# A two-layer gated cross-attention and expert kernel: another order for the two passages from attention to experts

## The reference, cut to what matters

```python
x = x + tanh(g_xattn[0]) * L0_xattn(layernorm(x), ctx)         # 8 heads of 64
x = x + tanh(g_ffn[0])   * L0_experts(layernorm(x))            # silu(a) * b, biases, top 2 of 8
x = x + tanh(g_xattn[1]) * L1_xattn(layernorm(x), ctx, ctx)    # 16 heads of 8
x = x + tanh(g_ffn[1])   * L1_experts(layernorm(x))            # gelu, top 2 of 8
```

## Time and profile before

| | |
|---|---|
| median of 3 runs | 788.54 us (787.5 to 790.2) |
| profiled execution | 795.85 us, of which the span of the instructions is 794.1 us |
| granted TensorE clock, mean | 0.933 |
| busy share of the span | PE 81%, DVE 70%, POOL 56%, ACT 56% |
| layer 0 attention | row minima from 36.2 to 232.1 us |
| layer 0 experts | first block's PE product at 247.5 us, last store at 419.7 us |
| layer 1 attention | row maxima from 414.9 to 640.7 us |
| layer 1 experts | first block's PE product at 655.5 us, last store at 779.0 us |

### The profile page before, as it was taken

How to read it: one execution, slowest core, us unless ns; L and a number is a source line. 1 busy time by engine, 2 the same in 40 slices (tenths; PEclk the granted TensorE clock), 3 DMA queues, 4 the chain that set the end, 5 groups by cost and what they waited for, 6 DMA issues and landing times.

```text
span 794.1 us, 16522 instructions
## 1 busy us (share of the span) xinstructions
PE 647.0 (81%) x4501; PEld 584.0 (74%) x4501; DVE 556.0 (70%) x1971; ACT 442.0 (56%) x1275; POOL 448.4 (56%) x665
## 2 busy tenths in 40 slices
PE   6888888899766767978688899889879875898886
PEld 5677778888666657877677788878768874787775
DVE  3367688887874566876787889888878755444564
ACT  2476767677434434655556776767665542433452
POOL 4035357776667565875445334767656665565541
PEclk9999999998978788999997999999999996999999
DMA  9446667454422223434352435535413013332444
GB/s 261 117 115 171 174 172 182 124 154 110 127 72 87 62 79 113 110 93 119 106 156 76 114 78 107 122 85 103 113 58 84 31 34 93 102 89 79 135 145 153
DMA packets 127383, 89.48 MB, mean 113 GB/s; under 512 B 30996, under 2 KB 116276, under 8 KB 127260
## 3 DMA queue, kind: packets, MB, share of 16 engines
q1 hardware_dynamic: 110844, 64.93, 32.1%
q0 software_dynamic: 8128, 17.65, 6.8%
q10 hardware_dynamic: 8320, 5.85, 2.6%
HBM read 50.73 MB, written 39.85 MB: 114 GB/s over the span
## 4 chain that ended last, share of the span: by engine, by line
PE 39%; DVE 21%; issue 12%; ACT 11%; SPq 5%; another core or an unknown queue 4%; DMA 3%; POOL 2%; DVEq 1%; ACTq 0%; POOLq 0%
PE banks L1171 7%; PE banks L1191 5%; PE banks L1034 5%; SPq L824 3%; DMA v_rows<-vo 3%; DVE row_max L1428 3%; PE banks L914 2%; PE banks L1001 2%; PE banks L977 2%; PE banks L1212 2%; PE banks L1019 2%; DVE hidden L1743 2%; DVE up L1735 2%; DVE x_res L1767 2%
## 5 line engine op out<-in xcount | busy, mean ns | idle before, releaser
L1925 POOL DMA_INDIRECT y_rows<-y_sb,result_at x134 | 131.1, 978 | 107.9 <-DVE result_at L1723 46.5
L1171 PE MATMUL banks<-xb,up 128*128 128x128 f32 x820 | 127.8, 297 | 47.1 <-DVE hidden L1743 22.4
L1171 PEld LDWEIGHTS banks<-xb,up 128*128 128x128 f32 x820 | 112.8, 207 | 61.5 <-issue 33.7
L1918 POOL DMA_INDIRECT x_rows<-xm,row x120 | 120.5, 1004 | 31.6 <-issue 28.5
L1880 POOL TENSOR_TENSOR v_flat<-v_raw,row_head 104x64 f32<-104x64 f32 (+1 forms) x128 | 55.6, 461 | 73.1 <-ACT v_raw L1345 72.1
L1191 PE MATMUL banks<-down,hidden 128*128 x536 | 87.6, 289 | 8.9 <-DVE y_sb L1760 4.6
L1329 ACT ACTIVATE prob_t<-banks 128x512 f32<-128x512 f32 x192 | 73.3, 439 | 28.7 <-PE banks L1001 24.8
L1034 PE MATMUL banks<-v_flat,prob_t 128*128 128x108 f32 (+2 forms) x640 | 86.5, 284 | 3.3 <-ACT prob_t L1329 1.3
L1034 PEld LDWEIGHTS banks<-v_flat,prob_t 128*128 128x128 f32 (+1 forms) x640 | 79.7, 197 | 10.6 <-ACT prob_t L1329 6.8
L1383 ACT ACTIVATE gate<-banks,block_bias 128x128 f32<-128x128 f32 x142 | 44.4, 365 | 76.2 <-PE banks L1171 44.7
L1191 PEld LDWEIGHTS banks<-down,hidden 128*128 128x128 f32 x536 | 75.0, 202 | 12.0 <-issue 12.0
(11 more groups left out here) (238 smaller groups left out, 1657.9 us busy)
## 6 DMA issues: line engine op xcount, KB each, us to landing
vo_flat<-v_rows SPq DMA_DIRECT2D x32, 256.0 KB
x_norm<-x_rows SPq DMA_DIRECT2D x74, 72.0 KB
v_rows<-vo SPq DMA_DIRECT2D x38, 128.0 KB
x_far<-x_rows SPq DMA_DIRECT2D x60, 72.0 KB
gathered<-y_rows ACTq DMA_DIRECT2D x32, 128.0 KB
q_rows<-up_raw SPq DMA_DIRECT2D x8, 512.0 KB, 2.8
q_even<-q_rows SPq DMA_DIRECT2D x12, 256.0 KB
q_odd<-q_rows SPq DMA_DIRECT2D x12, 256.0 KB
```

What stands on the lines that cost most here:

```text
L1171: done = pe.matmul(banks[:, UP_BANK[i % 2], part * P:(part + 1) * P], block_w[:, i % WR, part // 2, part % 2 * P:(part % 2 + 1) * P], xb[: ...
L1918: pool.indirect_dma_start(out=x_rows[layer][:, :], out_offset=bass.IndirectOffsetOnAxis(ap=row[:, n, c:c + 1], axis=0), in_=xm[:, i % 2, j ...
L1925: pool.indirect_dma_start(out=y_rows[layer][:, :], out_offset=bass.IndirectOffsetOnAxis(ap=result_at[:, i % (2 * YR):i % (2 * YR) + 1], ax ...
```

## The change

Only places in the task list change; no instruction is added or removed. With g for the group:

- Layer 0, part 0: totals from u = 27 to 28; the pieces of the table from 28, 28, 28 to 29, 30, 30; the bias product from 29 to 31.
- Layer 0, leads: group 5 from u = 32 to 35, group 6 from 35 into the experts' list, group 7 later in that list. In the list the order before is route tasks of group 7, totals, scatters, lead, three pieces with the last scatters between them, bias. After: the same without the lead, then bias, lead 6, lead 7 (steps 24 and 26 in place of 15 for lead 7).
- Layer 1, part 0: totals from u = 44 to 45; the pieces from 45, 45, 45 to 46, 47, 48.
- Layer 1, scatters of group 5: from u = 61, 62, 63, 64 to 61, 64, 64, 64.
- Layer 1, part 1: totals from u = 66, and the three pieces from u = 67, into the experts' list: totals at s = 5, pieces at 7, 9 and 11, between the tasks of the dense group. Group 6's lead goes from u = 67 to s = 13.
- Layer 1, dense group: its statistics from s = 5 to u = 68; its lead and `expert_w` from s = 15 to 14. The list no longer has rests in layer 1.

```diff
@@ expert_steps
-            rest = step[-1][0] != "scatter"
+            rest = layer == 0 and step[-1][0] != "scatter"
@@ order
-    steps0 = [((0, 1, 2, 3, 4, 5, 6), (5, 6, 7, 8))] * 5 + [((0, 1, 2, 3, 4, 5, 6), (5, 6, 7, 8)), ((0, 1, 2, 3, 3, 4, 5), (5, 5, 5, 5)), ((0, 1, 2, 3, 4, 5, 6), (5, 6, 7, 8))]
-    steps1 = [((0, 1, 3, 5, 6, 7, 9), (9, 11, 13, 15))] * 5 + [((0, 1, 3, 5, 6, 7, 9), (8, 9, 10, 11)), ((0, 1, 2, 3, 4, 5, 6), (6, 6, 7, 7)), ((0, 1, 3, 5, 6, 7, 9), (9, 11, 13, 15))]
-    tasks = [route_tasks(0, GS, 6, steps0, ((5, (6, 6, 6), 7), (5, (6, 6, 6), 7))),
-             route_tasks(1, 2 * GS, 13, steps1, ((7, (8, 8, 8), 0), (5, (6, 6, 6), 0)))]
+    steps0 = [((0, 1, 2, 3, 4, 5, 6), (5, 6, 7, 8))] * 5 + [((0, 1, 2, 3, 4, 5, 9), (5, 6, 7, 8)), ((0, 1, 2, 3, 3, 4, 14.5), (5, 5, 5, 5)), ((0, 1, 2, 3, 4, 5, 10.6), (5, 6, 7, 8))]
+    steps1 = [((0, 1, 3, 5, 6, 7, 9), (9, 11, 13, 15))] * 5 + [((0, 1, 3, 5, 6, 7, 9), (8, 11, 11, 11)), ((0, 1, 2, 3, 4, 5, 17), (6, 6, 7, 7)), ((-1, 1, 3, 5, 7, 0, 9), ())]
+    tasks = [route_tasks(0, GS, 6, steps0, ((6, (7, 8, 8), 9), (6, (7, 8, 9), 10))),
+             route_tasks(1, 2 * GS, 13, steps1, ((8, (9, 10, 11), 0), (8, (10, 12, 14), 0)))]
```

## The result

The change makes the kernel faster, by half of what was forecast: 787.11 us median (779.07 to 789.25, 20 runs) against 790.02 us (786.11 to 795.53, 20 runs), ratio 0.9942, 95% interval 0.9919 to 0.9965. The ratio is that of the means (785.77 and 790.34 us): 4.6 us less, with 1.9 either way. The medians differ by 2.9 alone, since after has a tail of short executions, down to 779.07. Timed twice more, each time beside the kernel before on one chip, the same kernel had 0.9942 (0.9917 to 0.9967) and 0.9963 (0.9940 to 0.9986).

The account below looks back on a forecast made before the run. No engine fills the span (PE 81%, DVE 70%), so waits that change by stage bound the kernel. Terms -1.4, 0, -3.0 and -4.2 sum to -8.6 us: 787.2 from the profiled 795.85, carried to the median 779.9; range 771 to 790.

Parts of the forecast that it names:

- the tables of layer 1: Layer 1's attention, part 0: totals and pieces moved into steps with waits, plus 0.5 for PE's clock; -3.0 us, ends -5.9 and 0.
- the passage: Layer 1, from last attention steps into the experts: four terms, -1.6, -4.1, +1.5 and 0, summing to -4.2 us.
- (a): Layer 1 passage: with group 5's scatters behind the last values, PE's product starts 1.6 us earlier; ends 0 and -1.6.
- (c): Layer 1 experts, steps 5 to 11: the moved 5.9 us of totals and pieces mostly fit DVE's free time; +1.5, ends 0 and 5.9.
- Layer 0: -1.4: End of layer 0's attention: totals, pieces and bias moved later, sum -1.4 us, ends -2.9 and +1.5.
- experts 0 (+-2): Layer 0's experts: scatters, pieces and bias one step earlier, leads 6 and 7 later; 0 us, ends -2 and +2.
- (d): Layer 1 experts: no rests, earlier expert_w and later leads touch nothing waited for before step 21's dense products; 0 us.
- trains of scatters: Rival, layer 1 passage: a train of six scatters holds PE's results, rank 2.5 us later; 792.5 us, slower; chance 0.15.
- (b): Layer 1 passage: without the lead behind totals, POOL starts group 6's eight scatters 4.1 us earlier; -4.1, bounds -6 and +1.
- shut out by DVE: Rival, layer 1 experts: POOL's stores grow beside DVE's table instructions, at most 1.7 us lost; 781.6 us; chance 0.03.
- Given back: Rival: gains hold up to the last attention step, but (b) is 0 and (c) is 4; 786.5 us; chance 0.17.
- more: Rival, layer 1: split train releases PE's results 6 us earlier and (c) is free; -12.0, with table ends 775; chance 0.15.

Follow-up runs that it names:

- 790 sets: The timed sets, the result among them, in which the kernel before takes 790 to 794 us; the 790 level is theirs.
- pair of traces: The two profiled executions against each other: kernel before 795.85 us, changed kernel 787.56 us.
- 745 sets: The two follow-up sets, first and fourth, in which the same kernel before takes 745 us.
- second set: Follow-up runs of the changed kernel and three variants of it, beside a kernel before of 792.17 us; the changed kernel 0.9942.
- third and fifth set: Third: variants combined, and group 6's lead by itself, kernel before 794.34 us. Fifth: changed kernel again (0.9963), and with totals at u = 44 (0.9943), kernel before 794.08.
- s3: Kernel before with layer 1's part 0 pieces at u = 46, 47, 48 and totals left at u = 44: 742.62 us, ratio 0.9954.
- p2: Kernel before with only layer 1's part 0 tables moved (totals u = 45, pieces 46, 47, 48): 744.78 us, ratio 0.9994.
- p3: Kernel before with the passage of layer 1 alone changed: 742.19 us, ratio 0.9956.
- s2: Kernel before with all of layer 1's part of the change, layer 0 as before: 739.81 us, ratio 0.9925.
- p4: Changed kernel with group 5's scatters back at one pair a step, u = 61 to 64: 740.71 us, ratio to before 0.9958.
- s4: Kernel before with layer 1's part, but totals at u = 44 and scatters of groups 5 and 6 one pair a step: 740.39 us, ratio 0.9947.
- q4: Changed kernel with scatters one pair a step, group 5's at u = 61 to 64, group 6's at 67 to 70: 785.72 us, ratio to before 0.9920.
- r1: Changed kernel with layer 1's part 0 totals at u = 44 and scatters of groups 5 and 6 one pair a step: 789.61 us, ratio to before 0.9947.
- r2: Changed kernel with layer 1's part 0 totals at u = 44 and only group 5's scatters one pair a step: 789.66 us, ratio to before 0.9947.
- r3: Kernel before with one task moved, group 6's lead from u = 67 into the experts' list: 791.32 us, ratio 0.9970.
- q1: The changed kernel timed once more, beside a kernel before of 792.17 us: 788.23 us, ratio 0.9942.

## Why the prediction was right in direction and wrong in size

The forecast was a gain of 8.6 us. Measured are 4.6 by the means and 2.9 by the medians, at the 790 level. So of the 7.2 us between 779.9 and 787.11 5.7 are gain that did not come, and 1.5 is the base: the median of before was 788.54 in the three runs shown and 790.02 in the twenty. The step that failed for certain is in the tables of layer 1; in the 790 sets two terms of the passage, (a) and (c), were too good as well. By the traces of the 790 sets the tables are worth 1.3 us (row maxima 44 to 50, means of six and of two traces) and the passage 2.1 (134.0, the mean of six, against the one trace of before); layer 0 is 2.1 shorter or 1.4 longer by the set. Each of these means has a spread as large as itself.

**Layer 0: -1.4, right for where it was made.** u = 27 to 29 lose 2.0, 1.1 and 1.4 in the pair of traces (steps of 5.0, 6.8 and 5.7 against 7.0, 7.9 and 7.1), 4.5 together where I had 5.0. u = 30 gains 1.9, where I had 2.1, and the row minimum of u = 31 comes 2.5 earlier, counted from u = 27. The bias wait then took 1.38 at the rank, where I had 1.5; net -1.3 at the first up product. In the 745 sets 1.4 are kept at block 40 (mean of 124.3 to 122.9). In the result and the second set it is more (148.3 in the mean against 150.2), in the third and fifth set nothing is kept (149.9 to 153.9 against 150.6): "experts 0 (+-2)" was the weak term there. I have not shown what holds them up, since those two sets have one trace with the order of before.

**Layer 1, tables: -3.0, mis-sized; -1.6 is what this order gave.** The step that failed is "totals stand at u = 45, of the kind whose next row maximum waits 0.99: 0.7 is left". The product of totals takes the bank that `rows1` uses at the odd steps, and waits on PE until ACT has copied v_raw. The score products stand behind it, so the spare 0.99 is never reached. I had listed who waits for a moved instruction on its queue, not who owns its bank. s3 confirms that the place of totals is the cause: one step earlier, in a step that I had read as full, the same tables take 3.2 off the attention in place of 1.6, and 0.9954 in place of 0.9994. That it is the bank is read from the releasers of the waits (0.47 on PE and 1.68 on DVE in after, 0.74 on DVE in p2), and was not tested with totals in another bank. So the step that I had read as full was the better place: with totals left there the tables give about the 3.0 of the forecast (3.2 in the trace, 3.4 by the ratio). In the pair of traces the steps 44 to 50 lose 1.9, but the whole attention takes 0.5 more (226.2 against 225.7): up to u = 44, where nothing was moved, after took 1.8 longer. The 0.5 for the clock is not told apart from this.

**Layer 1, passage: -4.2, right in the 745 sets, too much in the 790 ones.** In the former the last y_sb comes 4.2 earlier after the last row maximum (119.0 to 114.8 in the mean, with values 2.6 and 1.8 apart, and p3's 0.9956 is 3.3 us). That this is the forecast's own number is in part luck, since (a) and (d) are both off. In the latter 136.1, of one trace, becomes 131.4 in the pair, 133.2 in the mean of the result's and the second set's traces, and 135.6 in the fifth set's. By its terms:
- (a) -1.6. In the 745 sets it gives more: from the last row maximum to the first up product 16.0, 15.6, 14.7 and 16.0 in the order of before and 12.8 twice (p3, s2) with the train of six; with group 5's pairs apart 15.6 (p4) and 17.4 (s4). In the 790 sets 14.8 and 15.1 become 15.2 or 15.3 in three traces and 16.4 to 16.9 in four: nothing, or a loss. With the pairs apart it is 14.9, 14.9 and 17.4 (q4, r1, r2). DVE's "remote" waits of 3.0 us and more before L1505 stand in all seven traces with the train of six, and in none of the three without it: the train takes back what the earlier product gives. My rival *trains of scatters* had the mechanism and too high a price, 2.5 later; it is 0.4 in the pair of traces.
- (b) -4.1. r3 alone: last y_sb 3.1 earlier after the last row maximum, in one trace against one, and 0.9970, that is 2.4 (0.2 to 4.6). The term has the right sign, and its size lies below the forecast or at it.
- (c) +1.5, and (d) 0. The lead of 10.0 at the second y_sb is 2.1 at the tenth: steps 5 to 11 take back 7.9, not the 1.5, against 5.9 that I had moved there. In part that may be no loss: in before the blocks behind the held one came quickly after it. This is (c)'s share of the shortfall at the 790 level. In the 745 sets the lead of about 8 at the second y_sb is still there at the tenth, and half of it goes in the next ten, which take 20.4 and 19.0 in place of 15.4. There stands the expert_w of step 14, a part of (d). DVE in p3 and then in p2:
```profile
649.83 0.29 DVE L1616 TENSOR_TENSOR hot_w<-hot,token_w 128x32 f32<-128x32 f32 x2 [5.83 <-POOL token_w L1908]
```
```profile
650.98 0.29 DVE L1616 TENSOR_TENSOR hot_w<-hot,token_w 128x32 f32<-128x32 f32 x2 [2.55 <-POOL token_w L1908]
```
The tanh is done at 644.23 in p3, but POOL's queue still holds the stores of the blocks ahead. They follow each other every 1.27 us there, which makes POOL the bound, and `expert_w` one step earlier is only a longer wait, by 3.3 us. Where to put it was not tried.

Of the rivals, *shut out by DVE* is not borne out: the mean store took 978 ns before and 986 after, which makes 1 us of POOL's time in 134 stores; the longest grew from 1.207 to 1.467 us, far from the five times of that rule. The longest store grew in a 745 set too (1.560 us in p3). Nor were all 134 stores beside a weight copy of DVE, as the prediction says: in the trace of before 91 overlap one, with a mean of 985 ns, and the other 43 have 965. *Given back* (786.5) came nearest to the time, but not by its mechanism: it had the tables whole and (b) at nothing. One figure of the prediction is a slip: *more* with the ends of layer 1's tables is 773.6, not 775.

## What the runs showed of the hardware

The same kernel before is 45 us or more shorter in some sets than in others, and nearly all of it is in the experts' steps: layer 1's attention takes 225.2 to 225.7 us in either. The traces differ in one thing throughout. Idle time that ends "remote" stands in each of the twelve traces of the 790 sets, 37 to 76 us of it on DVE and ACT together, and in none of the eight of the 745 sets. It shows where POOL issues indirect DMAs in a row. The first blocks of layer 0, order of before, ACT at the 790 level (the profile of before):
```profile
253.98 0.61 ACT L1383 ACTIVATE gate<-banks,block_bias 128x128 f32<-128x128 f32 x2
259.99 0.62 ACT L1383 ACTIVATE gate<-banks,block_bias 128x128 f32<-128x128 f32 x2 [4.92 <-remote]
```
and the same in a 745 set (p2, in which layer 0 is that of before):
```profile
254.62 0.62 ACT L1383 ACTIVATE gate<-banks,block_bias 128x128 f32<-128x128 f32 x2 [0.30 <-PE banks L1171]
256.06 0.62 ACT L1383 ACTIVATE gate<-banks,block_bias 128x128 f32<-128x128 f32 x2 [0.35 <-PE banks L1171]
258.41 0.62 ACT L1383 ACTIVATE gate<-banks,block_bias 128x128 f32<-128x128 f32 x2 [1.25 <-PE banks L1171]
259.86 0.62 ACT L1383 ACTIVATE gate<-banks,block_bias 128x128 f32<-128x128 f32 x2 [0.35 <-PE banks L1171]
```
In both POOL issues eight scatters, 1.27 us apart (251.34 to 261.3 and 248.38 to 258.4), and then stores. In the 745 set a block passes every 1.4 to 2.4 us beside them. At the 790 level PE's product for the gate at 259.99 is over at 254.52 + 1.13 = 255.65, by the profile's model of its end, and ACT starts 4.3 later; PE in the profile of before:
```profile
254.52 1.13 PE L1171 MATMUL banks<-xb,up 128*128 128x128 f32 x8 [1.11 <-DVE hidden L1743]
```
The same at the passage, six scatters ahead of DVE's L1505: 3.00 and 3.02 us "remote" (after, q1), 0.68 us in a 745 set (p3):
```profile
619.27 0.26 DVE L1505 RECIPROCAL inv_sum<-banks 128x16 f32<-128x16 f32 x1 [0.68 <-PE banks L1034]
```
Over the whole kernel, the idle time of ACT before its gates (busy and mean, then idle time), before at the 790 level and p2 in a 745 set:
```profile
L1383 ACT ACTIVATE gate<-banks,block_bias 128x128 f32<-128x128 f32 x142 | 44.4, 365 | 76.2 <-PE banks L1171 44.7 <-remote 18.4 <-issue 9.4
```
```profile
L1383 ACT ACTIVATE gate<-banks,block_bias 128x128 f32<-128x128 f32 x142 | 44.3, 363 | 44.6 <-PE banks L1171 37.9 <-DVE hidden L1743 3.6 <-DMA y_rows<-y_sb,result_at 3.0
```
What makes the one level or the other, whether it belongs to a chip or to a time, and what holds the results, is not shown. POOL's scatters themselves take as long in both (a median of 966 ns in before and 967 in p2).

## What to carry to other kernels

Before moving an instruction into a step with spare time, name the owner of the bank that it writes in that step, and what stands behind it in the queue; spare time that is seen on one engine is lost if another engine's wait comes first. Where the trace has "remote" waits beside rows of indirect DMAs, as here, a gain there may be worth less than its rows, and differ from one set of runs to another: time the kernel before beside every variant, on the same chip and in the same rounds. And when the profiled execution lies outside the timed ones, take differences of stretches that repeat between traces, not of the two profiled times.
